# Gate and up weights as the rows divided by their last group's scale, and both f16 halves of h on GpSimd

## What is computed

```python
x = x + layernorm(attention(layernorm(x)))       # 16 heads of 32, ALiBi, causal
x = x + layernorm(ffn(layernorm(x)))
def ffn(x):                                      # I = 1408, H = 512, GROUP_SIZE = 128
    w_gu   = fp4_value(gate_up_packed) * repeat(gate_up_scales, 128)   # [2 * I, H]: 4 groups a row
    w_down = fp4_value(down_packed) * repeat(down_scales, 128)         # [H, I]: 11 groups a row
    gate, up = split(x @ w_gu.T)
    h = silu(gate) * up
    y = h @ w_down.T
    return y / sqrt(mean(y * y) + 1e-6)
```

## Time and profile before

| | us |
|---|---|
| median of 3 runs | 2501.1 (2500.99 to 2502.26) |
| profiled execution, device time | 2504.12 |
| its span in the trace | 2502.4 |
| TensorE busy | 2428.5 (97%) |
| VectorE busy | 1546.9 (62%) |
| ScalarE busy | 1386.6 (55%) |
| GpSimd busy | 648.1 (26%) |
| mean granted TensorE clock | 0.986 of full |

### The profile page before, as it was taken

One profiled execution on the slowest core, in us unless ns is written; L12 is line 12 of the kernel. 1 busy time (PEld: TensorE's weight loads), 2 busy tenths in 40 slices (PEclk: granted clock), 3 DMA queues, 4 the chain that ended last, 5 costly groups with the idle time before them and its releaser, 6 DMA issues.

```text
span 2502.4 us, 39040 instructions
## 1 busy us (share of the span) xinstructions
PE 2428.5 (97%) x13372; PEld 1116.9 (45%) x13372; DVE 1546.9 (62%) x4344; ACT 1386.6 (55%) x3867; POOL 648.1 (26%) x904
## 2 busy tenths in 40 slices
PE   7689999999999999999999999999999999999988
PEld 3344444444444444444444444444444444444433
DVE  7856575666656656575665657566665665657442
ACT  4646556464655646566564655646465564646610
POOL 3412313122231312223132232312223131222312
PEclk9699999999999999999999999999999999999999
DMA  5020121201112030121202012120111203012000
GB/s 146 19 55 14 52 51 35 68 18 47 40 44 59 27 76 19 35 52 42 61 19 70 16 52 51 35 68 18 47 39 43 59 27 74 20 35 52 25 11 17
DMA packets 99525, 108.93 MB, mean 44 GB/s; under 512 B 22895, under 2 KB 73199, under 8 KB 99311
## 3 DMA queue, kind: packets, MB, share of 16 engines
q1 hardware_dynamic: 98462, 105.65, 16.2%
q10 hardware_dynamic: 864, 0.79, 0.1%
HBM read 38.49 MB, written 16.78 MB: 22 GB/s over the span
## 4 chain that ended last, share of the span: by engine, by line
PE 91%; DVE 3%; ACT 3%; POOL 1%; issue 1%; DMA 0%; ACTq 0%; POOLq 0%; DVEq 0%; SPq 0%
PE dense L364 66%; PE psO L567 6%; PE psO L364 4%; PE score L551 4%; PE low L534 3%; PE score L534 3%; PE low L551 1%; ACT arena L754 1%; PE low L370 1%; PE low L459 1%; PE score L459 1%; PE score L370 1%; POOL arena L1269 1%; ACT low L672 0%; DVE arena L957 0%
## 5 line engine op out<-in xcount | busy, mean ns | idle before, releaser
L364 PE MATMUL dense<-arena,wgu 128*128 128x512 f16 x4224 | 999.8, 379 | 0.9 <-DVE arena L916 0.9
L364 PEld LDWEIGHTS dense<-arena,wgu 128*128 128x128 f16 x4224 | 405.2, 97 | 427.9 <-issue 7.5
L364 PE MATMUL dense<-wdn,arena 128*128 128x512 f16 x2112 | 530.5, 380 | 2.6 <-POOL arena L1206 2.6
L1206 POOL TENSOR_TENSOR arena<-late,arena 128x512 f16<-128x512 f32 x176 | 203.5, 1157 | 923.3 <-DVE arena L950 765.2
L1116 DVE CUSTOM_DVE_ANT_0 low<-low,mmax 128x128 f32<-128x128 f32 (+3 forms) x672 | 277.9, 434 | 231.7 <-PE low L534 227.7
L754 ACT ACTIVATE arena<-score 128x512 f32<-128x512 f32 (+3 forms) x720 | 300.9, 438 | 193.6 <-PE score L551 149.4
L672 ACT ACTIVATE low<-low,ncol 128x128 f32<-128x128 f32 (+3 forms) x672 | 299.9, 446 | 145.2 <-DVE ncol L1116 136.3
L672 ACT ACTIVATE score<-score,ncol 128x384 f32<-128x384 f32 x352 | 214.2, 609 | 177.9 <-DVE ncol L1116 177.6
L1116 DVE CUSTOM_DVE_ANT_0 score<-score,mmax 128x384 f32<-128x384 f32 x352 | 214.3, 648 | 128.0 <-PE score L534 127.6
L364 PEld LDWEIGHTS dense<-wdn,arena 128*128 128x128 f16 x2112 | 199.1, 98 | 190.0 <-issue 11.4
L1269 POOL TENSOR_SCALAR_AFFINE_SELECT arena<-arena 128x512 f32<-128x512 f32 x240 | 157.2, 658 | 239.6 <-ACT arena L754 239.3
(11 more groups left out here) (163 smaller groups left out, 2904.0 us busy)
## 6 DMA issues: line engine op xcount, KB each, us to landing
qst<-arena SPq DMA_DIRECT2D x384, 64.0 KB, 2.0
kst<-arena SPq DMA_DIRECT2D x186, 128.0 KB, 2.6
xin<-x SPq DMA_DIRECT2D x16, 1024.0 KB, 5.2
late<-x SPq DMA_DIRECT2D x64, 256.0 KB, 2.8
out<-late SPq DMA_DIRECT2D x64, 256.0 KB, 2.0
qst<-mrow SPq DMA_DIRECT2D x96, 8.0 KB, 1.9
wgu<-wo_t SPq DMA_DIRECT2D x1, 1024.0 KB, 13.2
wgu<-wq_down SPq DMA_DIRECT2D x1, 768.0 KB, 4.5
```

The source lines that it names most:

```text
L364: ins = nc.tensor.matmul(dst, w, a, start=first and k == 0, stop=last and k == len(tt) - 1)
L1206: nc.gpsimd.tensor_tensor(ht[:, 1, m, :], tb[:, m % 2, :], ht[:, 0, m, :], ALU.subtract).then_inc(sem["hl"], 1)
```

## The change

**Gate and up weights.** Each row of gate and up is divided by a number of its own, `divisor`: the scale of its last group, or that scale times a power of two where the other scales are much larger. What is left in the last group are fp4 values times a power of two, which an f16 holds exactly, so that the group's low half is zero. It is neither stored nor multiplied: `wgu` loses one of 8 pieces, `GU_PRODUCTS` goes from 12 to 11, and the last piece has two matmuls (its weights by the high and by the low half of x). The divisor comes back where gate and up are read anyway: as the scale of `tanh` (`gate_scale`) and as the scalar of `up` (`h_scale`), now a column of 128 numbers in place of a constant. GpSimd computes them in `divisors()`, 19 instructions at the start of step 0, and the scales that VectorE converted in `decode(2)` with them. The low half of a gate or up unit on VectorE has 3 pieces in place of 4.

**h.** `h_split` on GpSimd writes the high half with a `tensor_scalar` and then the low half as before; VectorE's `h_high` is gone. GpSimd waits for `up(m)`, and for the DMAs that `h_high` waited for.

**Tables.** `F_FIRST` goes from 24 to 22, `LN1_SLOT` from 44 to 43.

```diff
-S_X, S_W, S_WQ, S_W4 = 2.0 ** 4, 2.0 ** 8, 2.0 ** 6, 2.0 ** 6
+S_X, S_W, S_WQ, S_W4, S_GU = 2.0 ** 4, 2.0 ** 8, 2.0 ** 6, 2.0 ** 6, 2.0 ** 4
-LN1_SLOT = 44
+LN1_SLOT = 43
-GU_PRODUCTS = 3 * KC
+GU_PRODUCTS = 3 * KC - 1
+LIFT = 8
-F_FIRST = 24
+F_FIRST = 22
...
-        wgu = sb("wgu", [P, 2, KC, 2 * I], f16)
+        wgu = sb("wgu", [P, 2 * KC - 1, 2 * I], f16)
...
             def ffn_up(m, up, a, b):
-                    tt = terms(lambda s, c: wgu[:, s, c, col:col + P], lambda s, c: x2t[:, s, c, :], KC)
+                    tt = terms(lambda s, c: wgu[:, KC * s + c, col:col + P], lambda s, c: x2t[:, s, c, :], KC - 1)
+                    tt += [(wgu[:, KC - 1, col:col + P], x2t[:, s, KC - 1, :]) for s in range(2)]
...
             def tanh(m):
                     nc.scalar.activation(tb[:, m % 2, :], bank(t, n)[:, :], ACT.Tanh,
-                                         scale=0.5 / (S_X * S_W4)).then_inc(sem["tanh"], 1)
+                                         scale=gate_scale[:, m:m + 1]).then_inc(sem["tanh"], 1)
...
             def decode(piece):
-                    ts(sc32[:, 0:2 * MI * GROUPS], sc16[:, 0:2 * MI * GROUPS], FP8_SCALE * S_W4, None,
-                       ALU.mult).then_inc(s_bits, 1)
...
             def unit(u):
+                groups = KC - 1 if u < 2 * MI else 4
-                nc.vector.scalar_tensor_tensor(unit_dst(u, 1), bank_, 1.0, unit_dst(u, 0),
+                nc.vector.scalar_tensor_tensor(unit_dst(u, 1), bank_[:, 0:groups, :], 1.0, unit_dst(u, 0)[:, 0:groups, :],
                                                ALU.mult, ALU.subtract).then_inc(s_prep_lo, 1)
...
             def up(m):
-                    nc.vector.scalar_tensor_tensor(tb[:, m % 2, :], tb[:, m % 2, :], S_H / (2 * (S_X * S_W4) ** 2),
+                    nc.vector.scalar_tensor_tensor(tb[:, m % 2, :], tb[:, m % 2, :], h_scale[:, m:m + 1],
                                                    bank(t, n)[:, :], ALU.mult, ALU.mult).then_inc(sem["freev"], 1)
-                def h_high(m):
-                    taken(dve, t, job_f(t, m, 1))
...
-                    nc.vector.tensor_scalar(ht[:, 0, m, :], tb[:, m % 2, :], 1.0, None, ALU.mult).then_inc(sem["hh"], 1)
...
         def _(pool):
+            def divisors():
+                scales16 = sc16[:, 0:2 * MI * GROUPS].rearrange("p (u g) -> p u g", g=GROUPS)
+                scales = sc32[:, 0:2 * MI * GROUPS].rearrange("p (u g) -> p u g", g=GROUPS)
...
+                put(nc.gpsimd.tensor_tensor(divisor[:, :], last, power2, ALU.mult))
+                put(nc.gpsimd.tensor_tensor(inverse, divisor[:, :], inverse, ALU.pow))
+                put(nc.gpsimd.tensor_tensor(scales, scales, inverse.unsqueeze(2).broadcast_to([P, 2 * MI, GROUPS]),
+                                            ALU.mult), False)
...
-                def h_low(m):
+                def h_split(m):
+                    taken(pool, t, job_f(t, m, 1))
...
+                    nc.gpsimd.tensor_scalar(ht[:, 0, m, :], tb[:, m % 2, :], 1.0, None, ALU.mult).then_inc(sem["hh"], 1)
                     pool.wait_ge(sem["hh"], val("hh", t, m + 1))
                     nc.gpsimd.tensor_tensor(ht[:, 1, m, :], tb[:, m % 2, :], ht[:, 0, m, :],
                                             ALU.subtract).then_inc(sem["hl"], 1)
```

More of the change, by code:

```diff
@@ L203, in layer_program @@
         half = sb("half", [P, NT], f32)
+        sizes = sb("sizes", [P, 2 * MI, GROUPS], f32)
+        pos_part = sb("pos_part", [P, 2 * MI, GROUPS], f32)
+        rows_of = sb("rows_of", [P, 4, 2 * MI], f32)
+        logs = sb("logs", [P, 2, 2 * MI], f32)
+        divisor = sb("divisor", [P, 2 * MI], f32)
+        gate_scale = sb("gate_scale", [P, MI], f32)
+        h_scale = sb("h_scale", [P, MI], f32)
         st6 = {n: sb("st6_" + n, [P, NT, 6], f32) for n in ("ln1", "ln2", "ln3", "lo")}
@@ L336, in unit_dst @@
             if u < 2 * MI:
-                return wgu[:, s, :, P * u:P * u + P]
+                return wgu[:, KC * s:2 * KC - 1 if s else KC, P * u:P * u + P]
             return wdn[:, s, u - 2 * MI, :].rearrange("p (a b) -> p a b", a=4)
@@ L573, in step @@
                     for m in range(MI):
-                        ffn_up(m, 0, 0, 12)
-                        ffn_up(m, 1, 0, 12)
+                        ffn_up(m, 0, 0, GU_PRODUCTS)
+                        ffn_up(m, 1, 0, GU_PRODUCTS)
                     for i in range(NT):
@@ L700, in step @@
                     nc.scalar.activation(wo[:, 0, :, :], raw_wo, ACT.Copy, scale=S_W).then_inc(s_raw_hi, 1)
+                if isinstance(t, int) and t == 1:
+                    act.wait_ge(s_norm, 19)
                 if ffn:
@@ L1092, in step @@
                         up(m)
-                        h_high(m)
                     for i in range(NT):
@@ L1135, in step @@
                                 gate(m)
-                            if slot == up_done(m, 1) + 2:
-                                if m:
-                                    up(m)
-                                h_high(m)
+                            if m and slot == up_done(m, 1) + 2:
+                                up(m)
                         for i in range(NT):
@@ L1178, in unit @@
             def unit(u):
-                pool.wait_ge(s_bits, 7)
+                pool.wait_ge(s_bits, 6)
+                pool.wait_ge(s_norm, 19)
                 if u >= 2 * MI:
@@ L1189, in unit, with put @@
                                         ALU.mult).then_inc(s_blk, 1)
+            def divisors():
+                n = [0]
+                def put(ins, settle=True):
+                    n[0] += 1
+                    ins.then_inc(s_norm, 1)
+                    if settle:
+                        pool.wait_ge(s_norm, n[0])
+                scales16 = sc16[:, 0:2 * MI * GROUPS].rearrange("p (u g) -> p u g", g=GROUPS)
+                scales = sc32[:, 0:2 * MI * GROUPS].rearrange("p (u g) -> p u g", g=GROUPS)
+                wide, last, power2, inverse = (rows_of[:, k, :] for k in range(4))
+                pool.wait_ge(s_gu, 32)
+                put(nc.gpsimd.memset(inverse, -1.0), False)
+                put(nc.gpsimd.tensor_scalar(scales, scales16, FP8_SCALE * S_GU, None, ALU.mult), False)
+                put(nc.gpsimd.tensor_scalar(sizes[:, :, :], scales16, -1.0, 0.0, ALU.mult, ALU.max), False)
+                put(nc.gpsimd.tensor_scalar(pos_part[:, :, :], scales16, 0.0, None, ALU.max))
+                put(nc.gpsimd.tensor_tensor(sizes[:, :, :], sizes[:, :, :], pos_part[:, :, :], ALU.add))
+                put(nc.gpsimd.tensor_tensor(pos_part[:, :, 0:2], sizes[:, :, 0:2], sizes[:, :, 2:4], ALU.add), False)
+                put(nc.gpsimd.tensor_scalar(last, sizes[:, :, GROUPS - 1], 2.0 ** -26, None, ALU.max))
+                put(nc.gpsimd.tensor_tensor(wide, pos_part[:, :, 0], pos_part[:, :, 1], ALU.add))
+                put(nc.gpsimd.tensor_scalar(logs[:, :, :], rows_of[:, 0:2, :].bitcast(i32), 2.0 ** -23, None, ALU.mult))
+                put(nc.gpsimd.tensor_tensor(wide, logs[:, 0, :], logs[:, 1, :], ALU.subtract))
+                put(nc.gpsimd.tensor_scalar(wide, wide, 127.0 - LIFT, 127.0, ALU.add, ALU.max))
+                put(nc.gpsimd.tensor_scalar(power2.bitcast(i32), wide, 1.0, None, ALU.mult))
+                put(nc.gpsimd.tensor_scalar(power2.bitcast(i32), power2.bitcast(i32), 2.0 ** 23, None, ALU.mult))
+                put(nc.gpsimd.tensor_tensor(divisor[:, :], last, power2, ALU.mult))
+                put(nc.gpsimd.tensor_tensor(inverse, divisor[:, :], inverse, ALU.pow))
+                put(nc.gpsimd.tensor_tensor(scales, scales, inverse.unsqueeze(2).broadcast_to([P, 2 * MI, GROUPS]),
+                                            ALU.mult), False)
+                put(nc.gpsimd.tensor_scalar(gate_scale[:, :], divisor[:, 0:MI], 0.5 / (S_X * S_GU), None, ALU.mult))
+                put(nc.gpsimd.tensor_scalar(divisor[:, 0:MI], divisor[:, 0:MI], S_H / (2 * (S_X * S_GU) ** 2), None,
+                                            ALU.mult))
+                put(nc.gpsimd.tensor_tensor(h_scale[:, :], divisor[:, 0:MI], divisor[:, MI:2 * MI], ALU.mult))
@@ L1197, in step @@
                 n_y = (2 if ffn else 0) + (1 if nxt else 0)
-                def h_low(m):
+                def h_split(m):
+                    taken(pool, t, job_f(t, m, 1))
+                    if m in (0, 2) and att:
+                        name = "qstk0" if m == 0 else "qstk1"
+                        pool.wait_ge(sem[name], val(name, t, 192))
                     if m == 0 and att:
                         stacked_k(pool, t)
+                    nc.gpsimd.tensor_scalar(ht[:, 0, m, :], tb[:, m % 2, :], 1.0, None, ALU.mult).then_inc(sem["hh"], 1)
                     pool.wait_ge(sem["hh"], val("hh", t, m + 1))
@@ L1279, in step @@
                 if isinstance(t, int) and t == 0:
+                    divisors()
                     for u in range(RING):
```

17 lines of the change are left out of this document (6 added, 11 removed).

## The result

The changed kernel takes 2472.8 us (median) against 2501.7 for the kernel before on the same chip, a ratio of 0.9881 with a 95% interval of [0.9861, 0.99]: 1.2% faster. One of its four executions, of the slow state, took 6963.3 us for a reason that nothing here shows; the other three took 2471.5, 2471.6 and 2474.0 us, the ratio is worked out from these, and their own median is 2471.6. The prediction was 2472 us. The profiled execution after has a span of 2469.7 us against 2502.4, so the two traces differ by 32.7 us, of which the medians show 28.9 (30.1 with the median of the three).

What follows compares the result with a forecast made beforehand. The prediction took TensorE's work to bound steps 1 to 15. Its terms, -76.0 + 37.5 - 4.7 + 13.6 + 0.3 = -29.3 us, took 2501.1 to 2471.8 us, range 2448 to 2486.

Steps and rivals of the forecast that it cites:

- Matmuls, -76.0: TensorE, steps 1 to 16: 352 matmuls fewer at 0.2158 us each, all on the path, 76.0 us saved.
- The wait at set 5: PE waits for GpSimd's keep_causal(5), now queued behind rs_ln: 2.7 us in each of steps 1 to 14, +37.5 us.
- Set 9, -4.7: PE's 0.33 us wait at set 9 goes, since a power of y stands two slots sooner: 14 times, 4.7 us back.
- The clock, 8 of 14 times 1.7 = 13.6: PE falls to half clock behind 8 of 14 new waits, 1.7 us each: +13.6 us, bounds 0 and 24.
- The rule named beside it: Skill page's warning only of idle gaps longer than this one; by it PE's clock would hold and the term be 0.
- The high half, 0.65 us, +0.3: GpSimd's tensor_scalar on h takes 0.65 us, covered except at the end of step 16, which gets 0.3 us longer.
- the bound of 4.6: Upper end for GpSimd's high-half instruction, 4.6 us, scaled from a 128x32 tensor_scalar as if all its time were per element.
- What it might lose ScalarE makes good before PE needs it.: Tile 5's split on GpSimd, ahead of tanh(7): some tenths might be lost, but ScalarE recovers them before PE needs the result.
- divisors(), 0: Start of step 0: 19 small GpSimd instructions end near 33 us, hidden since PE takes the units only at 46.37; price 0.
- Step 0, 0 of -3 to +3: Rest of step 0: shorter VectorE low halves against a late keep_causal(5), taken as 0 in a range of -3 to +3 us.
- The rival without a wait: No wait at set 5, from sooner moments on VectorE or unseen slack: 2425 us, up to 2432; chance 0.08.

Runs made afterwards that it cites:

- e8: Changed kernel with rs_ln and first rs_lo behind keep_causal(6), first y_add behind keep_causal(7), tanh(7) behind row_copy(0): 2422.5 us, ratio 0.9679.
- e1: Changed kernel with the power rs_ln one slot later on GpSimd, behind keep_causal(5): 2445.0 us, ratio 0.9767 to the kernel before.
- e4: The kernel before with LN1_SLOT 43 in place of 44 and nothing else changed: 2553.1 us, ratio 1.02.
- e6: Changed kernel with the high half of h written by VectorE again, in the slots of the change: 2467.8 us, ratio 0.9861 to the kernel before.
- e7: e1 with GpSimd writing the high half of each h tile twice: 2472.3 us, 27.3 above e1.
- e11: Changed kernel with rs_ln and first rs_lo behind keep_causal(6) and tanh(7) one slot later, behind row_copy(0): 2436.8 us, ratio 0.9737 to the kernel before.
- e5: The kernel before with GpSimd writing both halves of h, weights and slots unchanged: 2503.9 us against 2502.9, ratio 1.0006.

## Why the prediction was right

- **Matmuls, -76.0.** Right. Step 15, which has neither the wait nor a fall, lost 4.8 us, and in e8 a step is 4.93 shorter with 5.08 due.
- **The wait at set 5, 14 times 2.68.** Right to hundredths, in place, cause and size: GpSimd's order (e1), and `LN1_SLOT` alone (e4).
- **Set 9, -4.7.** Right; the row is gone, and the power that held it runs earlier, as forecast.
- **The clock, 8 of 14 times 1.7 = 13.6.** This term was mis-sized: 3 times, 1.3 to 1.6 us, 4.4 in all. The price of a fall was near, the count was a guess between 0 and 14, and the runs show 3, 6 and 8 for waits within 0.2 us of each other. The rule named beside it, from the Trainium skill's page TensorE: Matmul & The Clock Gate, section Why this matters for your kernels, speaks of longer gaps alone and would have had 0. The runs disagree with it (17 falls in 42 waits of 2.4 to 2.9 us).
- **The high half, 0.65 us, +0.3.** Mis-sized: 1.49 us, and step 16 lost 1.2. The nearest rows, the select (0.64) and the subtraction (1.16), both lie below it. The step that failed is "I take 0.65, one input and the same size"; the bound of 4.6 held it.
- **"What it might lose ScalarE makes good before PE needs it."** This failed: 0.31 us in each of 15 steps, 4.6 us. The place was named, but it was left out that `tanh(7)` had moved ahead of `row_copy(0)` (`F_FIRST` 22), so that its delay passes into a DMA on which PE waits. e6, e7 and e11 show it.
- **divisors(), 0.** Right: they end at 35.99 instead of 33, and the units begin 2 us later (36.15 for 34.18 in the earlier trace rows), 9 us ahead of PE (45.17).
- **Step 0, 0 of -3 to +3.** +0.8.

Two errors of opposite sign, 9.2 us too much for the clock and 5.5 too little for the high half and what it holds up, and 0.8 of step 0, left the sum at -29.3 where the account has -32.2. The medians, with 28.9 (30.1 without the one long execution), happen to lie nearer; the agreement to 1 us is luck and not the precision of the terms. The rival without a wait, 2425 to 2432 us, is what the change is worth with the masks in time: e8, which also moves one `tanh`, has 2422.

## What to carry to other kernels

Before a slot number is moved, write out the in-order engine's queue around it: an instruction that waits for a late producer holds everything behind it, and here one power of 1.04 us, one place too early, ate half of the 76 us that 352 fewer matmuls had earned. Work that the bounding engine waits for goes ahead of work that has slack, and each such mend uncovers the next (set 6, then set 7), so the waits are read anew after each. Relieving an engine that does not bound (68 us off VectorE in e5) brings nothing, and what it adds elsewhere shows where a chain is bare, at the end of the last step, or where a new order leads from it to the bounding engine.
